# TensorE transposes are placed between the products of a group instead of behind it, in a fused GroupNorm, Hadamard and two-layer-MLP kernel

## The chip, the cores and the metric

One core of one Trainium2 chip. The time is device time in microseconds (us), the median of the runs of one kernel. PE is TensorE, ACT is ScalarE, DVE is VectorE and POOL is GpSimd. Each engine runs its own list of instructions in order and waits on semaphores; data in transit lies in PSUM banks, which PE writes and ACT and DVE read.

## The reference

The input x has shape (16, 192, 56, 56), float32. Two residual blocks follow each other; each normalises over 32 groups of 6 channels and then mixes the channels of every pixel.

```python
def _gn(v, G=32, eps=1e-05):
    B_, C_, H_, W_ = v.shape
    g = v.reshape(B_, G, C_ // G, H_, W_)
    m = jnp.mean(g, axis=(2, 3, 4), keepdims=True)
    s = jnp.var(g, axis=(2, 3, 4), keepdims=True)
    return ((g - m) / jnp.sqrt(s + eps)).reshape(v.shape)
...
x = x + _L0_conv_ref(_gn(x))      # y = xr padded to 256 @ hadamard / 16, first 192 columns
x = x + _L1_conv_ref(_gn(x), W1, b1, g1, beta1, W2, b2, g2, beta2, W3, b3)
...
# _L1_conv_ref, for each pixel, over its 192 channels:
h = jnp.einsum('bhwc,oc->bhwo', h, W1) + b1
h = jax.nn.gelu(_layernorm(h, g1, beta1), approximate=False)
h = jnp.einsum('bhwc,oc->bhwo', h, W2) + b2
h = jax.nn.gelu(_layernorm(h, g2, beta2), approximate=False)
h = jnp.einsum('bhwc,oc->bhwo', h, W3) + b3
```

## The kernel before, in words

Images are taken in 8 pairs. The 3136 pixels of a pair are cut into six units of 512 pixels; the 64 left over of each are collected into one more unit (g = 44), so there are 49. A unit holds 2 x 192 channels in three blocks of 128 partitions: a and b (128 channels of either image) and c (64 of each). Every float32 operand of a product is split into a float16 high and low part, so a product is two or three matmuls.

A unit goes through these pieces on PE, each a function of its code:

- `h_ab`, `h_c` (and `h_left` for the leftovers): Hadamard products, 512 columns wide, into the PSUM tile `hl` (banks "a" and "b"). DVE adds them to x (`residual`, L1089; `residual_left`, L1098).
- `group(g, n, h)`: layer n (0 or 1) of the MLP for half h of unit g: two bias products of 388 columns (L567), 12 pairs of 192 columns on 64 rows each (L573), 12 of 192 columns on 128 rows (L578), into `tm[h]`. Its output has pixels on the partitions. ACT squares it and sums the squares (L729), POOL makes the reciprocal root (L935), DVE multiplies (`normalise`, L1248) into `z[n]`.
- `transposes(g, n, h)`: six float32 transposes of 128 x 128 of `z[n]` (four, L590, into bank "tp0"; two, L597, into "tp1"), which bring the channels back to the partitions. The code calls layer 1 n = 0 and layer 2 n = 1. The first four wait until ACT has read what bank tp0 held. ACT applies gelu (L741 from tp0, L746 from tp1 after the second half) and makes the high part (`gelu_hi`, L759); POOL makes the low part (`gelu_lo`, L943).
- `l3_ab`, `l3_c`: the third product, 512 columns, again into `hl`. DVE adds it to x (`final_ab`, L1279; `final_c`, L1287), and it is stored. `l3_ab` waits for `gelu_lo` of the unit; `l3_c` waits until `final_ab` has read bank "a" (its first product is L511, its last L516).

`run` calls one function for each g on every engine: `first` for g below 6, `step` up to 41, `last` up to 47, `drain` for the rest. A step works on several units at once: layer 1 of unit g, layer 2 of unit g-1, the third product of unit g-2, the Hadamard product of unit g+7. Each sixth step collects statistics for a GroupNorm (`gn_means`, `h_shift`, `w1_shift`: small products into bank "b", with short DVE operations round them).

The lists of the other engines are fixed in the same way. In a step, ACT has: squares(g,0,0), gelu(g-2,1,1), the first high part of the next Hadamard input (xs_hi), gelu_hi(g-2,1,1), squares(g,0,1), two more xs_hi, squares(g-1,1,0), gelu(g,0,0), three high parts of the next layer 1 input (x_hi, L706), gelu_hi(g,0,0), squares(g-1,1,1), gelu(g,0,1), gelu_hi(g,0,1), gelu(g-1,1,0), gelu_hi(g-1,1,0). DVE has: statistics of x, residual, normalise(g,0,0), two more residuals with statistics, two xs_lo, normalise(g,0,1), one xs_lo, two low parts of the layer 1 input (L1230), final_ab(g-2), normalise(g-1,1,0), the third low part, statistics, normalise(g-1,1,1), final_c(g-2). POOL has: the root for (g,0,0), gelu_lo(g-2,1,1), roots for (g,0,1) and (g-1,1,0), gelu_lo(g,0,0), the root for (g-1,1,1), gelu_lo(g,0,1), gelu_lo(g-1,1,0).

## Time and profile before

| | |
|---|---|
| median of 3 runs | 927.61 us (927.29 to 929.92) |
| span of the profiled execution | 927.5 us |
| PE busy | 831.8 us, 90% |
| ACT busy | 814.3 us, 88% |
| DVE busy | 799.5 us, 86% |
| POOL busy | 551.2 us, 59% |
| granted TensorE clock, mean | 0.985 of full speed |

The profiled execution is one run with the profiler on; its own time is its span, within 0.1 us of the median, with nothing listed around it. A line such as "412.65 0.34 PE L567 ... x2" says that two instructions of line 567 start at 412.65 us and that the last ends 0.34 later. Matmuls are pipelined, so a matmul's duration is longer than the distance to the next one; the distance of starts is what a matmul costs.

### The profile page before, as it was taken

What the parts mean: (1) busy time and instruction counts of PE and PEld (TensorE: products, weight loads), DVE (VectorE), ACT (ScalarE), POOL (GpSimd) and SP (SyncE); (2) the same over time, 40 slices, a digit from 0 to 9 for tenths busy, and PEclk for the clock granted to TensorE, in tenths of its full rate; (3) what the DMA queues carried; (4) which work ended last, traced back from release to release, by engine and by line L of the source; (5) the groups of instructions that cost most, each with busy time, mean ns of one, the idle gap of its engine ahead of it and who ended that gap; (6) DMA issues with size and microseconds to landing.
All of it is one profiled execution on the core that took longest, in us unless ns stands there. A gap on an engine that the chain in (4) does not pass through costs nothing.

```text
span 927.5 us, 22221 instructions
## 1 busy us (share of the span) xinstructions
PE 831.8 (90%) x8353; PEld 552.3 (60%) x8353; DVE 799.5 (86%) x1416; ACT 814.3 (88%) x2400; POOL 551.2 (59%) x414
## 2 busy tenths in 40 slices
PE   0646889899999999999999999999999999889897
PEld 0114545556666666666666666666666667566663
DVE  6699898999999999999999999999998887745455
ACT  0687879689999999999999999999999998999982
POOL 0452544566666666666666666766766666577760
PEclk9987999999999999999999999999999999999999
DMA  9725022223323333233233232332111113121213
GB/s 265 234 69 145 1 70 69 74 69 104 107 69 108 103 105 98 81 103 108 70 110 101 94 117 70 98 113 84 59 40 55 50 36 104 40 69 35 70 36 102
DMA packets 52090, 81.99 MB, mean 88 GB/s; under 512 B 14608, under 2 KB 14736, under 8 KB 51856
## 3 DMA queue, kind: packets, MB, share of 16 engines
q1 hardware_dynamic: 51984, 80.58, 28.8%
q8 instruction: 67, 1.10, 0.5%
q14 instruction: 39, 0.32, 0.1%
HBM read 41.23 MB, written 39.32 MB: 87 GB/s over the span
## 4 chain that ended last, share of the span: by engine, by line
PE 48%; DVE 31%; ACT 10%; POOL 7%; issue 2%; SPq 1%; DMA 1%; ACTq 0%; DVEq 0%; POOLq 0%
PE tm L578 11%; DVE z L1248 6%; PE tm L573 5%; PE tp L590 5%; DVE X L1089 5%; DVE xs_lo L1080 4%; POOL ge_lo L943 4%; PE hl L487 4%; DVE bn L1106 3%; DVE x_lo L1230 3%; PE hl L418 3%; ACT z L729 3%; PE tm L567 3%; PE hl L516 2%; PE hl L492 2%; PE hl L511 2%
## 5 line engine op out<-in xcount | busy, mean ns | idle before, releaser
L943 POOL TENSOR_TENSOR ge_lo<-ge,ge_hi 128x512 f16<-128x512 f32 (+1 forms) x190 | 314.1, 1664 | 189.7 <-ACT ge_hi L759 189.7
L729 ACT ACTIVATE z<-tm 128x194 f32<-128x194 f32 x784 | 250.8, 346 | 41.9 <-PE tm L578 38.6
L935 POOL TENSOR_TENSOR rs<-ssq,neg_half 128x4 f32<-128x4 f32 x196 | 204.9, 1046 | 124.1 <-ACT z L729 123.2
L1248 DVE TENSOR_TENSOR z<-tm,rs 128x768 f32<-128x768 f32 x196 | 186.0, 949 | 62.1 <-POOL rs L935 61.3
L729 ACT ACTIVATION_READ_ACCUMULATOR z<-tm 128x1 f32 x784 | 175.1, 223 | 0.0
L741 ACT ACTIVATE ge<-tp,par 128x512 f32<-128x512 f32 x196 | 155.2, 792 | 21.1 <-PE tp L590 20.5
L759 ACT ACTIVATE ge_hi<-ge 128x512 f16<-128x512 f32 (+1 forms) x190 | 161.8, 855 | 2.9
L1089 DVE SCALAR_TENSOR_TENSOR X<-hl,h_bias,X 128x512 f32<-128x512 f32 x138 | 102.0, 741 | 30.6 <-PE hl L423 30.1
L590 PE MATMUL tp<-cst,z 128*128 128x128 f32 x784 | 121.8, 278 | 4.9 <-DVE z L1248 2.8
L1230 DVE SCALAR_TENSOR_TENSOR x_lo<-X,gscale,x_hi 128x512 f16<-128x512 f32 x144 | 102.8, 743 | 1.1 <-ACT x_hi L706 1.1
L590 PEld LDWEIGHTS tp<-cst,z 128*128 128x128 f32 x784 | 85.7, 142 | 28.4 <-issue 21.7
L706 ACT ACTIVATE x_hi<-X,gscale 128x512 f16<-128x512 f32 x144 | 95.7, 745 | 6.8 <-DVE gshift L1186 6.5
L578 PE MATMUL tm<-w_hi,ge_hi 128*128 128x192 f16 x392 | 98.0, 250 | 0.0
L1106 DVE BATCH_NORM_STATS2 bn<-X 128x6 f32<-128x512 f32 x144 | 97.6, 683 | 0.0
L578 PE MATMUL tm<-w_hi,ge_lo 128*128 128x192 f16 x392 | 97.0, 247 | 0.0
L578 PE MATMUL tm<-w_lo,ge_hi 128*128 128x192 f16 x392 | 97.0, 247 | 0.0
L578 PE MATMUL tm<-w_hi,x_hi 128*128 128x192 f16 x384 | 96.6, 252 | 0.0
L695 ACT ACTIVATE xs_hi<-X,gscale 128x512 f16<-128x512 f32 (+1 forms) x129 | 92.6, 767 | 4.4 <-DVE gscale L1177 4.4
L578 PE MATMUL tm<-w_lo,x_hi 128*128 128x192 f16 x384 | 95.7, 249 | 0.0
L578 PE MATMUL tm<-w_hi,x_lo 128*128 128x192 f16 x384 | 95.6, 249 | 0.0
L1080 DVE SCALAR_TENSOR_TENSOR xs_lo<-X,gscale,xs_hi 128x512 f16<-128x512 f32 (+1 forms) x129 | 92.9, 751 | 0.5 <-ACT xs_hi L695 0.4
L1066 DVE BATCH_NORM_STATS2 bn<-X 128x6 f32<-128x512 f32 x132 | 83.4, 677 | 4.8 <-DMA X<-x 4.7
(192 smaller groups left out, 1888.2 us busy)
## 6 DMA issues: line engine op xcount, KB each, us to landing
out<-X SPq DMA_DIRECT2D x48, 512.0 KB, 2.9
X<-x SPq DMA_DIRECT2D x40, 512.0 KB, 4.0
out<-X SPq DMA_DIRECT2D x98, 128.0 KB, 3.0
X<-x SPq DMA_DIRECT2D x80, 128.0 KB, 4.1
X<-x SPq DMA_DIRECT2D x8, 576.0 KB, 4.2
X<-x SPq DMA_DIRECT2D x16, 144.0 KB, 4.4
X<-weights SPq DMA_DIRECT2D x1, 1024.0 KB, 12.1
out<-X SPq DMA_DIRECT2D x8, 64.0 KB, 3.0
```

The lines of the kernel that those rows point to most:

```text
L578: last = nc.tensor.matmul(dst[:, i, k * TW:k * TW + C], tokens(act, slice(0, 128), i, k), w[:, 3 * i, :], start=False, stop=(r == 2), skip ...
L590: last = nc.tensor.transpose(tp[:, 0, i * HALF + k * TT:i * HALF + (k + 1) * TT], z[n][:, 2 * h + k, at:at + 128], ident[0:TT, 0:TT])
L729: last = nc.scalar.activation(z[n][:, 2 * h + k, i * TW:(i + 1) * TW], tm[h][:, i, k * TW:(k + 1) * TW], ACT.Square, scale=float(C) ** -0. ...
L741: nc.scalar.activation(ge[n][:, 2 * h:2 * h + 2, :], tp[:, 0, 0:2 * HALF].rearrange("p (b t) -> p b t", b=2), ACT.Gelu, bias=par[:, 4 * n ...
L759: nc.scalar.activation(ge_hi[n][:, g % 2, PART[h], :], ge[n][:, PART[h], :], ACT.Copy).then_inc(s_ge_hi[n], 1)
L935: nc.gpsimd.tensor_tensor(rs[n][:, 2 * h:2 * h + 2, :], ssq[n][:, 2 * h:2 * h + 2, :], neg_half[0:TT, 0:4].rearrange("p (i k) -> p i k", i=2),
L943: nc.gpsimd.tensor_tensor(ge_lo[n][:, g % 2, PART[h], :], ge[n][:, PART[h], :], ge_hi[n][:, g % 2, PART[h], :], ALU.subtract).then_inc(s_g ...
L1080: ins = nc.vector.scalar_tensor_tensor(out=xs_at(xs_lo, a, wide(a))[:, b, :], in0=xcols(a, b, wide(a)), scalar=scale1(a // U, b), in1=xs_a ...
L1089: nc.vector.scalar_tensor_tensor(out=xcols(a, b), in0=tp[:, 0, 0:UT] if b == 2 and a < U else hl[:, b % 2, 0:UT], scalar=h_bias[:, (a // U ...
L1106: ins = nc.vector.bn_stats(bn[1][:, (a // U) % 2, b, a % U, :], xcols(a, b))
L1230: ins = nc.vector.scalar_tensor_tensor(out=x1_lo[:, a % 2, b, :], in0=xcols(a, b), scalar=scale2(a // U, b), in1=x1_hi[:, a % 2, b, :], op ...
L1248: nc.vector.tensor_tensor(z[n][:, 2 * h:2 * h + 2, 0:2 * C].rearrange("p k (i o) -> p i k o", i=2), tm[h][:, :, 0:2 * TW].rearrange("p i ( ...
```

## The change

A new function `transpose(g, n, h, j)` does the j-th of the six transposes of `transposes(g, n, h)`, with the same waits and signals: the wait for z and for bank tp0 before the first, the signal to ACT after the fourth. `group`, `h_ab`, `l3_ab` and `l3_c` take a second set of numbers, `turned`, and place those six transposes between their own products. ACT, DVE, POOL and SP keep their lists. The lines of `drain` change only where g is 48; `first` leaves out its last transposes when g is 5, since step 6 now makes them.

```diff
-            def h_ab(a):
+            def h_ab(a, *turned):
...
                         nc.tensor.matmul(hl[:, i, 0:UT], h16[:, AA, :], part[:, i, :], start=(r == 0), stop=False,
                                          skip_group_check=True)
+                        if turned:
+                            transpose(*turned, 2 * i + r)
+                if turned:
+                    transposes(*turned, 4)
...
-            def l3_ab(g):
+            def l3_ab(g, *turned):
...
                         nc.tensor.matmul(dst[:, i], w[:, AA, :], act[:, i:4:2, :], start=(r == 0), stop=False,
                                          skip_group_check=True)
+                        if turned:
+                            transpose(*turned, 3 * i + r)
...
-            def l3_c(g):
+            def l3_c(g, *turned):
...
                     nc.tensor.matmul(dst, w[:, CCB, :], act[:, 4:6, :], start=(r == 0), stop=False,
                                      skip_group_check=True)
+                    if turned:
+                        transpose(*turned, 2 * r)
+                        transpose(*turned, 2 * r + 1)
...
-            def group(g, n, h):
+            def group(g, n, h, *turned):
...
+                            if turned and (3 * k + r) % 2 == 1 and (i, k, r) != (0, 1, 2):
+                                transpose(*turned, 3 * i + (3 * k + r) // 2)
                     last.then_inc(s_mm[n], 1)
-
-            def transposes(g, n, h):
+                    if turned and i == 0:
+                        transpose(*turned, 2)
+
+            def transpose(g, n, h, j):
+
+
+
                 if not 0 <= g < NL:
                     return
...
+                if j == 0:
+                    pe.wait_ge(s_z[n], 2 * g + h + 1)
+                    free("tp0")
+                if j < 4:
+                    k, i = divmod(j, 2)
+                    at = (0, C + CC)[i]
+                    last = nc.tensor.transpose(tp[:, 0, i * HALF + k * TT:i * HALF + (k + 1) * TT],
+                                               z[n][:, 2 * h + k, at:at + 128], ident[0:TT, 0:TT])
+                    if j == 3:
+                        last.then_inc(s_tp[n], 1)
+                        held["tp0"] = s_ge[n], 3 * g + h + 1
+                    return
+                k = j - 4
+                if k == 0 and h == 0:
                     free("tp1")
...
+            def transposes(g, n, h, first=0):
+                for j in range(first, 6):
+                    transpose(g, n, h, j)
...
             def step(g):
-                group(g, 0, 0)
-                transposes(g - 2, 1, 1)
-                h_ab(h_unit(g, 0))
+                group(g, 0, 0, g - 2, 1, 0)
+                h_ab(h_unit(g, 0), g - 2, 1, 1)
                 group(g, 0, 1)
...
                 h_left(h_unit(g, 0))
-                transposes(g, 0, 0)
-                l3_ab(g - 2)
+                l3_ab(g - 2, g, 0, 0)
                 group(g - 1, 1, 1)
-                transposes(g, 0, 1)
                 w1_shift(gn2_pair(g))
                 h_shift(h_shift_pair(g))
-                l3_c(g - 2)
-                transposes(g - 1, 1, 0)
+                l3_c(g - 2, g, 0, 1)
 
             def last(g):
-                group(g, 0, 0)
+                group(g, 0, 0, g - 2, 1, 0)
                 transposes(g - 2, 1, 1)
                 group(g, 0, 1)
                 group(g - 1, 1, 0)
-                transposes(g, 0, 0)
-                l3_ab(g - 2)
+                l3_ab(g - 2, g, 0, 0)
                 group(g - 1, 1, 1)
-                transposes(g, 0, 1)
-                l3_c(g - 2)
-                transposes(g - 1, 1, 0)
+                l3_c(g - 2, g, 0, 1)
```

The first place, on PE: the end of a plain step, from the last products of layer 2 to the first of the next unit's group. Before (L590 and L597 are transposes, L511 and L516 are l3_c, L567 is the next group):

```order
L578 MATMUL tm<-w_hi,ge_lo 128x192
L590 MATMUL tp<-cst,z 128x128 x4
L597 MATMUL tp<-cst,z 128x128 x2
L511 MATMUL hl<-ge_hi,w_hi 128x512
L511 MATMUL hl<-ge_lo,w_hi 128x512
L511 MATMUL hl<-ge_hi,w_lo 128x512
L516 MATMUL hl<-ge_hi,w_hi 64x512 x2
L516 MATMUL hl<-ge_lo,w_hi 64x512 x2
L516 MATMUL hl<-ge_hi,w_lo 64x512 x2
L590 MATMUL tp<-cst,z 128x128 x4
L597 MATMUL tp<-cst,z 128x128 x2
L567 MATMUL tm<-bias,ones 128x388 x2
```

The same place of the changed kernel (L619 and L628 are the transposes, L526 and L534 are l3_c, L588 the next group; in this step a w1_shift stands ahead):

```order
L526 MATMUL hl<-ge_hi,w_hi 128x512
L619 MATMUL tp<-cst,z 128x128 x2
L526 MATMUL hl<-ge_lo,w_hi 128x512
L619 MATMUL tp<-cst,z 128x128 x2
L526 MATMUL hl<-ge_hi,w_lo 128x512
L628 MATMUL tp<-cst,z 128x128 x2
L534 MATMUL hl<-ge_hi,w_hi 64x512 x2
L534 MATMUL hl<-ge_lo,w_hi 64x512 x2
L534 MATMUL hl<-ge_hi,w_lo 64x512 x2
L588 MATMUL tm<-bias,ones 128x388 x2
```

The six of layer 1's second half moved from ahead of l3_c to behind its first product; the six of layer 2 that stood between l3_c and the next group are gone from here.

The second place, on PE: the second part of group(g,0,0) and the start of h_ab. Before, the twelve L578 stood in a row, then six transposes, then h_ab:

```order
L578 MATMUL tm<-w_lo,x_hi 128x192
L578 MATMUL tm<-w_hi,x_lo 128x192
L590 MATMUL tp<-cst,z 128x128 x4
L597 MATMUL tp<-cst,z 128x128 x2
L418 MATMUL hl<-xs_hi,h 128x512
L418 MATMUL hl<-xs_lo,h 128x512
```

Now the last six of the twelve (L599), with four transposes among and before them, and then h_ab (L421):

```order
L619 MATMUL tp<-cst,z 128x128
L599 MATMUL tm<-w_hi,x_hi 128x192
L599 MATMUL tm<-w_lo,x_hi 128x192
L619 MATMUL tp<-cst,z 128x128
L599 MATMUL tm<-w_hi,x_lo 128x192
L599 MATMUL tm<-w_hi,x_hi 128x192
L628 MATMUL tp<-cst,z 128x128
L599 MATMUL tm<-w_lo,x_hi 128x192
L599 MATMUL tm<-w_hi,x_lo 128x192
L628 MATMUL tp<-cst,z 128x128
L421 MATMUL hl<-xs_hi,h 128x512
L619 MATMUL tp<-cst,z 128x128
```

Between the products of group(g,0,0) stand the six of layer 2's first half, which were behind l3_c; the six of its second half, which followed the group, now alternate with h_ab's four wide products.

The third place, on PE: l3_ab (L497), where six transposes (L619, L628) of layer 1's first half stood ahead of its first product and now alternate with it:

```order
L599 MATMUL tm<-w_hi,ge_lo 128x192
L497 MATMUL hl<-ge_hi,w_hi 128x512
L619 MATMUL tp<-cst,z 128x128
L497 MATMUL hl<-ge_lo,w_hi 128x512
L619 MATMUL tp<-cst,z 128x128
L497 MATMUL hl<-ge_hi,w_lo 128x512
L619 MATMUL tp<-cst,z 128x128
L497 MATMUL hl<-ge_hi,w_hi 128x512
L619 MATMUL tp<-cst,z 128x128
L497 MATMUL hl<-ge_lo,w_hi 128x512
```

The wait of l3_ab for POOL's low part now stands ahead of these transposes too.

## Rows read from the trace of the kernel before

**Rows 1.** The page: busy time, share of the span and instructions of each engine.
```profile
PE 831.8 (90%) x8353; PEld 552.3 (60%) x8353; DVE 799.5 (86%) x1416; ACT 814.3 (88%) x2400; POOL 551.2 (59%) x414
```

**Rows 2.** Waits of DVE, 190 to 720 us (us in total, times, longest).
```profile
DVE X L1089 <- PE hl L423: 15.9, 16, 2.9
```

**Rows 3.** Line L1279 over the span: who waited for it (us, times).
```profile
  PEld hl L511: 6.5, 16
```

**Rows 4.** Timeline of PE: first products of group(g,0,0) (start us, us, what).
```profile
412.65 0.34 PE L567 MATMUL tm<-bias,ones 64*128 64x388 f16 x2
...
428.65 0.34 PE L567 MATMUL tm<-bias,ones 64*128 64x388 f16 x2
...
444.54 0.34 PE L567 MATMUL tm<-bias,ones 64*128 64x388 f16 x2
...
462.01 0.34 PE L567 MATMUL tm<-bias,ones 64*128 64x388 f16 x2
...
479.25 0.34 PE L567 MATMUL tm<-bias,ones 64*128 64x388 f16 x2
...
497.77 0.34 PE L567 MATMUL tm<-bias,ones 64*128 64x388 f16 x2
...
844.19 0.34 PE L567 MATMUL tm<-bias,ones 64*128 64x388 f16 x2
...
859.34 0.34 PE L567 MATMUL tm<-bias,ones 64*128 64x388 f16 x2
```

**Rows 5.** Timeline of DVE, steps 19 and 22.
```profile
416.68 0.75 DVE L1089 SCALAR_TENSOR_TENSOR X<-hl,h_bias,X 128x512 f32<-128x512 f32 x1 [0.48 <-PE hl L423]
...
423.73 0.74 DVE L1230 SCALAR_TENSOR_TENSOR x_lo<-X,gscale,x_hi 128x512 f16<-128x512 f32 x1
...
425.05 1.21 DVE L1279 SCALAR_TENSOR_TENSOR X<-hl,X 128x1024 f32<-128x1024 f32 x1
...
471.47 0.66 DVE L1098 SCALAR_TENSOR_TENSOR X<-hl,h_bias,X 128x64 f32<-128x64 f32 x3
...
474.89 1.22 DVE L1279 SCALAR_TENSOR_TENSOR X<-hl,X 128x1024 f32<-128x1024 f32 x1
```

**Rows 6.** Timeline of PE, end of step 18 and step 19.
```profile
409.68 0.60 PE L590 MATMUL tp<-cst,z 128*128 128x128 f32 x4
...
410.33 0.38 PE L511 MATMUL hl<-ge_hi,w_hi 128*128 128x512 f16 x1
410.55 0.38 PE L511 MATMUL hl<-ge_lo,w_hi 128*128 128x512 f16 x1
...
411.53 0.38 PE L516 MATMUL hl<-ge_hi,w_lo 128*64 128x512 f16 x2
411.84 0.66 PE L590 MATMUL tp<-cst,z 128*128 128x128 f32 x4
412.34 0.38 PE L597 MATMUL tp<-cst,z 128*128 128x128 f32 x2
...
413.42 0.26 PE L578 MATMUL tm<-w_hi,x_hi 128*128 128x192 f16 x1
...
414.42 0.60 PE L590 MATMUL tp<-cst,z 128*128 128x128 f32 x4
...
419.31 0.34 PE L567 MATMUL tm<-bias,ones 64*128 64x388 f16 x2
```

**Rows 7.** Timeline of ACT and of POOL, step 19.
```profile
413.08 0.76 ACT L741 ACTIVATE ge<-tp,par 128x512 f32<-128x512 f32 x1
...
417.57 1.08 ACT L759 ACTIVATE ge_hi<-ge 128x1024 f16<-128x1024 f32 x1
...
422.17 0.86 ACT L741 ACTIVATE ge<-tp,par 128x512 f32<-128x512 f32 x1
...
422.83 0.81 ACT L706 ACTIVATE x_hi<-X,gscale 128x512 f16<-128x512 f32 x1
...
418.72 2.13 POOL L943 TENSOR_TENSOR ge_lo<-ge,ge_hi 128x1024 f16<-128x1024 f32 x1 [1.25 <-ACT ge_hi L759]
```

More of the change, by code:

```diff
@@ L584, in transposes @@
                     return
-                pe.wait_ge(s_z[n], 2 * g + h + 1)
-                done = 3 * g + h
-                free("tp0")
-                for k in range(2):
-                    for i, at in ((0, 0), (1, C + CC)):
-                        last = nc.tensor.transpose(tp[:, 0, i * HALF + k * TT:i * HALF + (k + 1) * TT],
-                                                   z[n][:, 2 * h + k, at:at + 128], ident[0:TT, 0:TT])
-                last.then_inc(s_tp[n], 1)
-                held["tp0"] = s_ge[n], done + 1
@@ L595, in transposes @@
+                k = j - 4
+                if k == 0 and h == 0:
                     free("tp1")
-                for k in range(2):
-                    last = nc.tensor.transpose(tp[:, 1, h * HALF + k * TT:h * HALF + (k + 1) * TT], z[n][:, 2 * h + k, CA:CA + 128],
-                                               ident[0:TT, 0:TT])
-                if h == 1:
+                last = nc.tensor.transpose(tp[:, 1, h * HALF + k * TT:h * HALF + (k + 1) * TT], z[n][:, 2 * h + k, CA:CA + 128],
+                                           ident[0:TT, 0:TT])
@@ L600, in transposes @@
+                if k == 1 and h == 1:
                     last.then_inc(s_tp[n], 1)
-                    held["tp1"] = s_ge[n], done + 2
+                    held["tp1"] = s_ge[n], 3 * g + 3
+            def transposes(g, n, h, first=0):
+                for j in range(first, 6):
+                    transpose(g, n, h, j)
             def first(g):
```

17 lines of the change are left out of this document (14 added, 3 removed).

## The prediction, written before the changed kernel was run

> **What bounds the kernel now.** I read the page first. PE, ACT and DVE are all busy for 86 to 90% of the span [rows 1], so shares alone name no bound. The reader should see there only that a gain on PE alone may be worth nothing.
>
> Then the waits. In the stretch of full steps (190 to 720 us) DVE has one wait of weight: for the last product of h_ab, before the first residual of a step, 15.9 us in 16 waits [rows 2]. The other side is in the waits of l3_c: its first weight load (L511) waits for final_ab (L1279) 16 times [rows 3]. So the two engines hand a baton round: PE's h_ab releases DVE's residual, DVE runs without a gap to final_ab, final_ab releases l3_c, and PE runs from l3_c through group(g,0,0) to the next h_ab.
>
> The timelines of one step show that this loop closes. I call S the start of group(g,0,0); step 19 has S = 412.65, and the next has 428.65, 16.00 later [rows 4]. Residual starts at S+4.03, final_ab ends at 425.05+1.21 = S+13.61 [rows 5]. In the step before, final_ab's waiter L511 starts at 410.33, 2.32 before S [rows 6]. 4.03 + 9.58 + 0.06 of handing over (L511 would start at S+13.67) + 2.32 = 15.99: the step. There is no slack in it. ACT is the other full engine: from the gelu at 413.08 on it has no gap in this step [rows 7].
>
> Of six steps (one pair of images) three are plain; the two of them in the rows last 16.00 and 15.89. The other three carry GroupNorm work and last 17.47, 17.24 and 18.52 [rows 4].
>
> **The cost of a transpose.** Six transposes before a 512-column product take 410.33 - 409.68 = 0.65, so 0.109 each; a 512-column product takes 0.217 (410.33 to 410.55), and twelve 192-column ones 1.00 (413.42 to 414.42), 0.083 each [rows 6]. A 512-column product behind a change of array shape (from 128 rows and columns to 64 rows or 64 columns, or back) comes 0.31 after the one before it, so a change costs 0.09. Four transposes behind such a change take 0.50 instead of 0.44 (411.84 to 412.34): an exposed float32 weight load costs 0.06. That is less than any product beside it, so the loads are hidden already, and alternating hides nothing more. The last of the six before L511 also keeps its 0.109 though a float16 load stands behind it, whereas 192-column products follow such loads at 0.083. I price an alternated transpose at 0.109. No row shows one between 512-column products; the bounds are 0.05 (if 0.06 is all that it needs) and 0.17 (0.109 plus an exposed load).
>
> The Trainium skill, "TensorE: Matmul & The Clock Gate", section "LDWEIGHTS (loading the stationary operand)", gives columns/1.2 ns, an estimate of 107 ns for these 128 columns: then transposes in a row are bound by their loads and alternating would pay. The row of the exposed load speaks against it; it is the third rival.
>
> **What the change saves.** The six transposes between l3_c and group(g,0,0) go. From the last pair of L516 (411.53) to S is 1.12 now; without them one change of array shape stays, priced as the one seen (411.53 to 411.84, 0.31). 1.12 - 0.31 - 0.65 (the six are done elsewhere) = 0.16 saved a step. If PE were the bound, 42 steps would give 7 us.
>
> **What it puts on the loop.** (1) transposes(g,0,1), 0.65, ran before l3_c's wait for final_ab, hidden. Now they stand behind l3_c's first product, so behind that wait. l3_c to S: 2.32 + 0.65 - 0.81 = 2.16. (2) The six that stood before S now stand inside group(g,0,0): h_ab, and with it the residual, comes at S+4.68, not 4.03. Together +0.49 a step. If DVE had a gap before final_ab, this would be covered; it has none.
>
> (3) Bank tp0. The gelu of transposes(g-2,1,0) must finish before transposes(g-2,1,1) may begin. Before, a whole group(g,0,0) stood between them. Now the fourth of the first six starts at S + 0.77 + 8 x 0.083 + 3 x 0.109 = S+1.76, ends 0.27 later (0.60 for four less three starts), ACT's gelu starts 0.05 behind that, at S+2.08, and lasts 0.76 [rows 7], and PE may go on at S+2.9. PE gets there at S + 0.77 + 1.00 + 0.65 + 0.22 = S+2.64. Stall and exposed load: 0.33. DVE is late next: residual at S+5.01.
>
> (4) ACT's queue. That gelu stood at 413.08 = S+0.43; now it can't be before S+2.08, and everything behind it in ACT's order follows at its old distance, since ACT has no gap. gelu_hi(g-2,1,1) started 4.49 after it (417.57), GpSimd's gelu_lo 5.64 after it and took 2.13 (418.72 to 420.85) [rows 7]. So l3_ab can't start before 2.08 + 7.77 + 0.06 = S+9.91; PE is there at S+9.41: group(g-1,1,0) starts at 419.31 = S+6.66 now, later by 0.65 and 0.33, and takes 1.77 (as 412.65 to 414.42 does). Stall 0.5, where now gelu_lo ends at 420.85 = S+8.2 and l3_ab starts at 6.66 + 1.77 + 0.65 = S+9.08.
>
> (5) transposes(g,0,0) ran before l3_ab and its wait; now they alternate with it. The fourth starts at 9.91 + 4 x 0.217 + 3 x 0.109 = S+11.11; 0.32 later, as in (3), gelu(g,0,0) starts, at S+11.43 (now 422.17 = S+9.52). Behind it in ACT's queue stand the three x_hi splits, 0.66 later (422.17 to 422.83) [rows 7], the first done 0.81 after its start, at S+12.90. DVE's x1 low parts (L1230) wait for it: they start at S+12.95 (now 423.73 = S+11.08; the loop alone would give 12.06). From there to the end of final_ab is 425.05 + 1.21 - 423.73 = 2.53 [rows 5], so l3_c starts at 12.95 + 2.53 + 0.06 = S+15.54 and the next step at +2.16: 17.7. A plain step goes from 15.9 to 17.7, +1.8. DVE's idle moves from the residual to x1_lo and POOL's chain; ACT gets gaps.
>
> The step with h_left (17.24): l3_ab there also waits for the leftover residual (L1098, 471.47 = S+9.46, three in 0.66) [rows 5]. That now comes at about 9.46 + 0.98 + 0.66 + 0.05 = S+11.15, and transposes(g,0,0) stand behind it: gelu at S+12.67, x_hi done at 14.14, final_ab at 14.19 + 2.53 = 16.72, then h_shift, which holds l3_c back by 17.24 - (474.89 + 1.22 - 462.01) - 2.32 = 0.82 [rows 4, 5] beyond final_ab, and 2.16: about 19.75, +2.5. In the other two, DVE has 1.5 to 2.6 us more of its own work in the step, which covers part of ACT's delay: between 0 and the plain 1.8; I take 0.75 each, about (1) to (3) alone.
>
> Six steps: 3 x 1.8 + 2.5 + 2 x 0.75 = 9.4. Steps 7 to 38 are 5.33 such sixes: 50. Steps 6 and 39 to 42 lie in between, one each: 5. The last plain ones (43 to 47, 844.19 to 859.34 = 15.15 [rows 4]) have no h work, but (3) and (4) hold on a loop of their own: l3_c to S 2.16, gelu 2.08, to gelu_lo's end and on 7.4 (7.83 less the xs split that ACT no longer has in between, some 0.4), l3_ab 2.7 (nine slots of 0.217, a change, six transposes), group(g-1,1,1) 1.77: 16.1, +0.9 each: 4. First steps (0 to 5) hardly change. Sum: +59. The profiled span is 927.5, 0.1 under the median of the runs, so I add to the median: 927.6 + 59, 986 us in whole numbers.
>
> **Rivals.**
> Second: (1) to (3) hold, but (4) and (5) are absorbed, because ACT's list has more give than one step shows. Then five of six steps gain 0.82 and one 0.1: 4.2 per six, 22, and 4 at the ends: 954. For it speaks that (4) and (5) are long sums of which each term must hold, and that ACT could gain a little where its operations are queued closely; against, that ACT shows no gap and its order is fixed.
> Third: alternated transposes cost 0.05, as if the load had been their price. 18 of them stand on loop (1) and (2), 12 on the way through (5): 0.65 less a step, 42 steps, 27 us less than the forecast: 959. That is where the page's rule would lead. Faster than before it does not become, since waits 3 to 5 stay.
> Fourth: only +0.49 holds, since gelu comes back in time: 2.5 per six and a little: 943.
> Fifth, other side: PE is the bound in practice and DVE catches up, because its waits before the residual (15.9 us) are slack and not part of the loop. Then 0.16 x 42 remain: 921. It decides if final_ab comes 0.65 earlier relative to PE; L511's 16 waits and the sum 15.99 speak against it.
> Sixth: the two cancel: 928.
>
> **How the numbers follow.** Chances: forecast 0.58, second 0.20, third 0.07, fourth 0.05, fifth 0.06, sixth 0.04. The forecast's own range is 968 to 1000 (each special step at its bounds, a transpose at up to 0.17). The range for all leaves out the fourth to sixth (0.15) and the upper tail: 945 to 997. A difference of 0.3% is about what can be told from no change. Slower 0.90, same 0.04, faster 0.06.
>
> **What the profile after would show.** Plain steps of 17.7, not 15.9. (1) L526 (l3_c) waiting for final_ab in nearly every step, for 1 us or more. (2) residual at S+5.0. (3) PE waiting about 0.3 for ACT's gelu in h_ab. (4) l3_ab waiting for GpSimd. (5) DVE waiting for x_hi before L1230. Transposes 0.109 after a 512-column product. Wrong would be: plain steps under 16.4, L526 without waits, or transposes at 0.05.

## The result, and the profile after

The kernel after takes 1001.42 us (median of 4 runs, 1000.71 to 1001.99) where the kernel before takes 927.45 beside it (926.90 to 929.92). The ratio is 1.079, 95% interval 1.077 to 1.081: 74 us slower. The forecast was 986 and the range 945 to 997, so the time lies outside it. The direction and most of the size came as written, and 15 us are left to explain.

The page of the kernel after: busy time and share of each engine, then the shares of the chain that ended last.

```profile
PE 839.8 (84%) x8353; PEld 569.8 (57%) x8353; DVE 822.9 (82%) x1416; ACT 821.8 (82%) x2400; POOL 560.7 (56%) x414
...
PE 33%; DVE 29%; ACT 19%; POOL 12%; issue 4%; SPq 1%; DMA 1%; ACTq 0%; DVEq 0%; POOLq 0%
```

Against [rows 1], no engine has much more work; all three full ones are idle for longer. DVE alone has 23 us more of busy time with the same 1416 instructions: some of them take longer than before, and the prediction had no such term.

Line numbers moved: h_ab is L421 and L430, l3_ab L497 and L504, l3_c L526 and L534, the group L588 to L599, the transposes L619 (tp0) and L628 (tp1), the gelu L773, x_hi L738, the residual L1121, the copy of GroupNorm means L1194, x1's low part (x_lo) L1262, final_ab L1311; POOL's root is L967, its gelu_lo L975. In the single-part kernels the numbers differ by one to three.

The waits, in the stretch 190 to 720 us (engine, line and who it waited for: us in total, times, longest):

```profile
ACT ge L773 <- PE tp L619: 65.5, 71, 3.1
DVE X L1121 <- PE hl L430: 28.2, 20, 2.7
...
PEld hl L526 <- DVE X L1311: 22.8, 20, 1.3
...
DVE x_lo L1262 <- ACT x_hi L738: 10.6, 9, 1.5
...
DVE z L1280 <- POOL rs L967: 5.6, 15, 2.3
...
PE hl L497 <- DVE gmu L1194: 4.4, 5, 0.9
PE hl L497 <- POOL ge_lo L975: 4.0, 14, 0.3
```

The reader sees ACT, which had no gap in step 19 [rows 7], wait 71 times for the transposes (6 times and 4.9 us in the kernel before); l3_c wait for final_ab by about 1.1 us each; and DVE's wait before the residual grow from 15.9 to 28.2 us [rows 2]. The 9 waits for x_hi stand one in each GN1 step (0.88) and one in each h_left step (1.54), none in a plain step; the kinds of step are explained at the table below. The last three rows are 15 waits for POOL's root (one, 0.6 us, in the kernel before), 5 for a copy of GroupNorm means and 14 of PE for gelu_lo; of the last two the kernel before has none.

The same plain step as in the prediction, step 19, first on PE (start us, us, what; in brackets the idle time before it and who ended it). S is 436.38.

```profile
436.38 0.34 PE L588 MATMUL tm<-bias,ones 64*128 64x388 f16 x2
...
439.38 0.30 PE L619 MATMUL tp<-cst,z 128*128 128x128 f32 x1 [0.20 <-ACT ge L773]
...
446.30 0.39 PE L497 MATMUL hl<-ge_hi,w_hi 128*128 128x512 f16 x1 [0.28 <-POOL ge_lo L975]
446.52 0.27 PE L619 MATMUL tp<-cst,z 128*128 128x128 f32 x1
446.63 0.38 PE L497 MATMUL hl<-ge_lo,w_hi 128*128 128x512 f16 x1
...
451.84 0.39 PE L526 MATMUL hl<-ge_hi,w_hi 128*128 128x512 f16 x1 [0.90 <-DVE X L1311]
...
454.01 0.34 PE L588 MATMUL tm<-bias,ones 64*128 64x388 f16 x2
```

The step is 454.01 - 436.38 = 17.63 long; it was 16.00 [rows 4]. A transpose between 512-column products costs 446.63 - 446.52 = 0.11, no less and no more than in a row [rows 6].

The other engines in the same step:

```profile
438.46 0.78 ACT L773 ACTIVATE ge<-tp,par 128x512 f32<-128x512 f32 x1 [0.64 <-PE tp L619]
...
447.81 0.78 ACT L773 ACTIVATE ge<-tp,par 128x512 f32<-128x512 f32 x1
448.49 1.94 ACT L738 ACTIVATE x_hi<-X,gscale 128x512 f16<-128x512 f32 x3
...
444.11 2.13 POOL L975 TENSOR_TENSOR ge_lo<-ge,ge_hi 128x1024 f16<-128x1024 f32 x1 [1.88 <-ACT ge_hi L791]
446.20 1.46 POOL L967 TENSOR_TENSOR rs<-ssq,neg_half 128x4 f32<-128x4 f32 x1
...
441.46 0.75 DVE L1121 SCALAR_TENSOR_TENSOR X<-hl,h_bias,X 128x512 f32<-128x512 f32 x1 [1.34 <-PE hl L430]
...
445.65 1.80 DVE L1112 SCALAR_TENSOR_TENSOR xs_lo<-X,gscale,xs_hi 128x512 f16<-128x512 f32 x2
447.69 0.96 DVE L1280 TENSOR_TENSOR z<-tm,rs 128x768 f32<-128x768 f32 x1 [0.23 <-POOL rs L967]
...
449.23 1.42 DVE L1262 SCALAR_TENSOR_TENSOR x_lo<-X,gscale,x_hi 128x512 f16<-128x512 f32 x2
```

Taken off S: the gelu at +2.08, the residual at +5.08, l3_ab at +9.92, the second gelu at +11.43, x1's low part at +12.85, l3_c at +15.46. Two of DVE's rows were not forecast. The pair of xs_lo takes 1.80 (1.40 in the kernel before), and the normalise behind it waits for a root that takes 1.46 and not 1.01.

Steps of all kernels, measured between first products of group(g,0,0) as in [rows 4]. "GN1" and "GN2" are the two steps of six that the prediction calls "the other two": GN1 collects the statistics for the first GroupNorm (steps 21, 27 and so on), GN2 those for the second (steps 23, 29). "Held" counts the xs_lo of over 0.9 us, of 153. Each ratio is to the kernel before as run beside that kernel, whose median lay between 927.45 and 929.21.

```
kernel       median   ratio [95%]             plain  GN1    h_left  GN2    43-47  held
before       927.45                           15.92  17.47  17.24   18.52  15.15    0
after       1001.42   1.079 [1.077, 1.081]    17.63  19.18  19.78   20.16  16.08   28
only_l3c     955.07   1.028 [1.025, 1.030]    16.77  17.63  17.63   19.42  15.30    0
only_l3ab    946.37   1.019 [1.017, 1.021]    16.28  18.44  18.42   18.68  15.23    0
only_g00     964.46   1.038 [1.036, 1.040]    16.97  17.56  17.98   19.90  15.43   23
only_hab     942.21   1.014 [1.011, 1.016]    16.39  17.47  17.93   18.93  15.16   23
undo_l3c     981.48   1.057 [1.055, 1.060]    16.99  18.55  19.13   19.91  16.10   23
undo_l3ab    988.94   1.066 [1.064, 1.067]    17.63  18.22  18.16   20.17  16.05   28
block_all    977.76   1.053 [1.051, 1.055]    17.10  18.61  19.25   19.54  15.47    0
early_xslo   933.59   1.006 [1.005, 1.008]    16.11  17.48  17.61   18.53  15.15   23
hab_clear    954.15   1.026 [1.024, 1.029]    17.02  17.48  18.30   19.50  15.16    5
block_only   944.15   1.016 [1.014, 1.017]    16.36  17.48  17.35   19.30  15.16   16
after_gn     998.06   1.074 [1.072, 1.075]    17.64  18.16  19.79   20.19  16.09   23
```

(Plain of before is the mean of 15.86, 16.00 and 15.89; plain of hab_clear is that of steps 18 and 19.)

### The profile page after: what moved, and what is told of

Its sections match the earlier page's. It is cut to its first block, busy times and chain, and to the rows that moved or that the text cites. A ratio compares the mean times of both kernels' runs of the same rounds, so it can differ in the third digit from the quotient of the medians.

```text
span 1000.2 us, 22221 instructions
## 1 busy us (share of the span) xinstructions
PE 839.8 (84%) x8353; PEld 569.8 (57%) x8353; DVE 822.9 (82%) x1416; ACT 821.8 (82%) x2400; POOL 560.7 (56%) x414
## 4 chain that ended last, share of the span: by engine, by line
PE 33%; DVE 29%; ACT 19%; POOL 12%; issue 4%; SPq 1%; DMA 1%; ACTq 0%; DVEq 0%; POOLq 0%
POOL ge_lo L975 7%; PE tm L599 6%; DVE x_lo L1262 6%; ACT ge L773 5%; ACT z L761 5%; PE tp L619 5%; DVE xs_lo L1112 5%; DVE X L1311 5%; POOL rs L967 5%; DVE z L1280 5%; PE tm L594 4%; PE hl L526 3%; PE hl L534 3%; ACT ge_hi L791 3%; PE hl L497 2%
## 5 line engine op out<-in xcount | busy, mean ns | idle before, releaser
L975 POOL TENSOR_TENSOR ge_lo<-ge,ge_hi 128x512 f16<-128x512 f32 (+1 forms) x190 | 312.1, 1654 | 280.5 <-ACT ge_hi L791 280.5
L967 POOL TENSOR_TENSOR rs<-ssq,neg_half 128x4 f32<-128x4 f32 x196 | 215.1, 1098 | 99.0 <-ACT z L761 93.1
L773 ACT ACTIVATE ge<-tp,par 128x512 f32<-128x512 f32 x196 | 153.2, 782 | 104.6 <-PE tp L619 103.4
L619 PE MATMUL tp<-cst,z 128*128 128x128 f32 x784 | 185.7, 276 | 14.6 <-ACT ge L773 13.7
L1121 DVE SCALAR_TENSOR_TENSOR X<-hl,h_bias,X 128x512 f32<-128x512 f32 x138 | 102.0, 741 | 52.6 <-PE hl L430 52.4
L619 PEld LDWEIGHTS tp<-cst,z 128*128 128x128 f32 x784 | 106.0, 141 | 41.8 <-issue 27.0
L1262 DVE SCALAR_TENSOR_TENSOR x_lo<-X,gscale,x_hi 128x512 f16<-128x512 f32 x144 | 103.1, 745 | 15.1 <-ACT x_hi L738 14.9
L1112 DVE SCALAR_TENSOR_TENSOR xs_lo<-X,gscale,xs_hi 128x512 f16<-128x512 f32 (+1 forms) x129 | 105.0, 843 | 1.2 <-ACT xs_hi L727 1.0
L738 ACT ACTIVATE x_hi<-X,gscale 128x512 f16<-128x512 f32 x144 | 94.4, 715 | 7.8 <-DVE gshift L1218 7.8
L599 PE MATMUL tm<-w_hi,ge_hi 128*128 128x192 f16 x392 | 98.0, 250 | 0.0
L1138 DVE BATCH_NORM_STATS2 bn<-X 128x6 f32<-128x512 f32 x144 | 97.6, 683 | 0.0
L599 PE MATMUL tm<-w_hi,ge_lo 128*128 128x192 f16 x392 | 96.9, 247 | 0.0
L599 PE MATMUL tm<-w_lo,ge_hi 128*128 128x192 f16 x392 | 96.9, 247 | 0.0
L599 PE MATMUL tm<-w_hi,x_hi 128*128 128x192 f16 x384 | 96.4, 251 | 0.0
L599 PE MATMUL tm<-w_hi,x_lo 128*128 128x192 f16 x384 | 95.4, 249 | 0.0
L599 PE MATMUL tm<-w_lo,x_hi 128*128 128x192 f16 x384 | 95.4, 249 | 0.0
L628 PE MATMUL tp<-cst,z 128*128 128x128 f32 x392 | 89.0, 273 | 0.0
```

Of the source, the lines that this page charges most:

```text
L599: last = nc.tensor.matmul(dst[:, i, k * TW:k * TW + C], tokens(act, slice(0, 128), i, k), w[:, 3 * i, :], start=False, stop=(r == 2), skip ...
L619: last = nc.tensor.transpose(tp[:, 0, i * HALF + k * TT:i * HALF + (k + 1) * TT], z[n][:, 2 * h + k, at:at + 128], ident[0:TT, 0:TT])
L773: nc.scalar.activation(ge[n][:, 2 * h:2 * h + 2, :], tp[:, 0, 0:2 * HALF].rearrange("p (b t) -> p b t", b=2), ACT.Gelu, bias=par[:, 4 * n ...
L967: nc.gpsimd.tensor_tensor(rs[n][:, 2 * h:2 * h + 2, :], ssq[n][:, 2 * h:2 * h + 2, :], neg_half[0:TT, 0:4].rearrange("p (i k) -> p i k", i=2),
L975: nc.gpsimd.tensor_tensor(ge_lo[n][:, g % 2, PART[h], :], ge[n][:, PART[h], :], ge_hi[n][:, g % 2, PART[h], :], ALU.subtract).then_inc(s_g ...
L1112: ins = nc.vector.scalar_tensor_tensor(out=xs_at(xs_lo, a, wide(a))[:, b, :], in0=xcols(a, b, wide(a)), scalar=scale1(a // U, b), in1=xs_a ...
```

## The experiments

**Each part alone.** Four kernels take the kernel before and one place of the change. The diffs show `step`; `last` has the same edit where it has these lines.

```diff
 # only_l3c
-                transposes(g, 0, 1)
...
-                l3_c(g - 2)
+                l3_c(g - 2, g, 0, 1)
 # only_l3ab
-                transposes(g, 0, 0)
-                l3_ab(g - 2)
+                l3_ab(g - 2, g, 0, 0)
 # only_g00 (and the six behind l3_c go)
-                group(g, 0, 0)
+                group(g, 0, 0, g - 2, 1, 0)
 # only_hab
-                transposes(g - 2, 1, 1)
-                h_ab(h_unit(g, 0))
+                h_ab(h_unit(g, 0), g - 2, 1, 1)
```

> Only the six transposes of layer 1's second half alternate with l3_c; the other three groups of six stay where the kernel before has them. Loop theory: these six now stand behind l3_c's wait for final_ab, and that wait ends each step's loop in the kernel before, so each of the 33 steps with index 6 to 38 and the few after it is longer by 0.65 to 0.7 us: plain steps 16.6, 955 us (950 to 960). Theory that alternating itself is dear on PE (the 74 us lost are spread over the four alternated groups alike): 946 us, and transposes further apart than 0.109 us behind a 512-column product. Theory that the waits do not matter: 928.

> Only the six of layer 1's first half alternate with l3_ab. Loop theory: gelu(g,0,0) comes 0.4 us later, and behind it in ACT's list x_hi, for which DVE's low part waits before final_ab: plain steps 16.3; the step with h_left +1.7, because the six now stand behind the leftover residual; the step with gn1 statistics +0.4, the one with gn2 statistics 0. Sum some 20 us: 948 (940 to 954). Theory that alternating itself is dear: 946, with all six kinds of step longer by the same 0.4.

> Only the first six of layer 2 move from behind l3_c into group(g,0,0); the other three groups stay in a row. Loop theory: one change of array shape less (0.16 saved), but h_ab comes 0.65 later, PE waits some 0.5 for bank tp0, and ACT's gelu can't start before 2.08 us after the step's start, which delays POOL's low part, POOL's root and DVE's normalise: plain steps 16.8 to 17.0, 967 us (960 to 975). Theory that alternating itself is dear: 946 or less. Theory that PE's own work is the bound: 921.

> Only the six of layer 2's second half alternate with h_ab; h_ab starts 0.65 earlier and ends when it did. Loop theory: no transpose moves behind a wait that binds, only gelu(g-2,1,1) comes 0.3 us later, and with it ACT's list: plain steps 16.0 to 16.2, 934 us (928 to 940), the smallest of the four. Theory that alternating itself is dear: 946.

Measured: 955.07, 946.37, 964.46 and 942.21. The first three are within 3 us of what was expected: putting six transposes behind l3_c's wait, behind l3_ab's wait, or ahead of a gelu that must come early, each costs time by itself. Alternating with h_ab, which has no such wait in front, was expected to cost least and did, but cost twice the expected: 942, not 934, and outside the 928 to 940 that was given. The four add up to 26 + 17 + 35 + 13 = 91 us against 74 together, so they share part of their cost.

**The miss of only_hab.** Its plain step, DVE and POOL:

```profile
421.48 0.75 DVE L1123 SCALAR_TENSOR_TENSOR X<-hl,h_bias,X 128x512 f32<-128x512 f32 x1 [0.45 <-PE hl L430]
...
425.52 1.62 DVE L1114 SCALAR_TENSOR_TENSOR xs_lo<-X,gscale,xs_hi 128x512 f16<-128x512 f32 x2
427.38 0.96 DVE L1282 TENSOR_TENSOR z<-tm,rs 128x768 f32<-128x768 f32 x1 [0.24 <-POOL rs L969]
...
430.24 1.22 DVE L1313 SCALAR_TENSOR_TENSOR X<-hl,X 128x1024 f32<-128x1024 f32 x1
...
423.80 2.14 POOL L977 TENSOR_TENSOR ge_lo<-ge,ge_hi 128x1024 f16<-128x1024 f32 x1 [1.75 <-ACT ge_hi L793]
425.89 1.46 POOL L969 TENSOR_TENSOR rs<-ssq,neg_half 128x4 f32<-128x4 f32 x1
```

From the residual's start to final_ab's end DVE needs 430.24 + 1.22 - 421.48 = 9.98, where it needed 9.58 before. The first xs_lo starts at 425.52, inside a gelu_lo that ends at 425.94. The root starts while that xs_lo runs and takes 1.46. In the kernel before, the gelu_lo ended (420.85 [rows 7]) before the pair began:

```profile
420.88 1.40 DVE L1080 SCALAR_TENSOR_TENSOR xs_lo<-X,gscale,xs_hi 128x512 f16<-128x512 f32 x2
```

So the pair takes 0.22 longer in only_hab, 1.62 for 1.40. The theory: an xs_lo and a POOL operation exclude each other, and the later one waits. The next kernel makes only that collision, with no transpose moved.

```diff
 # early_xslo: the kernel before, and in DVE's list
-                stats_x1(h_unit(g, 0), 1)
                 scaled_lo(xs_unit(g, 0), 0)
+                stats_x1(h_unit(g, 0), 1)
```

> The kernel before with two neighbours on DVE swapped in each full step: the first low part of the Hadamard input (xs_lo, two inputs in SBUF) stands ahead of the second statistics of x1, so it starts 0.6 us earlier, while POOL's gelu_lo still runs. Nothing is moved on PE, ACT or POOL. Theory that these two shut each other out: xs_lo takes 1.1 to 1.3 instead of 0.74 in most steps, POOL's root behind it 1.4, plain steps 16.3, 942 us (935 to 948). Theory that the long xs_lo of the changed kernel have another cause: 928.

```profile
421.17 1.02 DVE L1115 SCALAR_TENSOR_TENSOR xs_lo<-X,gscale,xs_hi 128x512 f16<-128x512 f32 x1
...
419.51 2.13 POOL L978 TENSOR_TENSOR ge_lo<-ge,ge_hi 128x1024 f16<-128x1024 f32 x1 [1.25 <-ACT ge_hi L794]
421.60 1.46 POOL L970 TENSOR_TENSOR rs<-ssq,neg_half 128x4 f32<-128x4 f32 x1
```

Same operations, same shapes: xs_lo goes from 0.74 to 1.02 (0.98 to 1.14) and the root behind it from 1.01 to 1.46, in 23 steps. The collision is real, and its whole price on this loop is 0.2 a plain step and 0.6% in all. I had expected 942 (935 to 948), 14 us over the kernel before, and it is 5.4 over the 928.15 beside it: I had the cause right and its size some 2.5 times too large.

The converse was tried on only_hab: DVE's third group of statistics goes from the step's start, where DVE waits, to just ahead of the first xs_lo, so that xs_lo starts behind gelu_lo.

```diff
 # hab_clear: only_hab, and in DVE's list
-                stats_part(g, 2)
...
                 stats_x1(h_unit(g, 0), 1)
+                if gn1_pair(g) is None:
+                    stats_part(g, 2)
                 scaled_lo(xs_unit(g, 0), 0)
```

> The kernel with only h_ab's alternation, and one more edit: DVE's third stats_part, 0.60 us, is taken from the step's start, where DVE waits, and put just ahead of the first xs_lo (except in the steps with statistics of GroupNorm 1, which need it). So xs_lo starts 0.60 later, behind the end of GpSimd's gelu_lo and the start of the root. If an xs_lo that starts inside a gelu_lo is what holds both back, then xs_lo falls from 0.96 to 0.74, the root from 1.46 to 1.01, and DVE's way from the residual to final_ab is 9.58 + 0.60 = 10.18 where it was 9.98 with the hold: plain steps of 16.6, about 948 in all, slower than 942 because the loop now carries work that the wait had covered. The rival, that gelu_lo and the root are only late and slow by themselves, keeps both durations and gives 9.98 + 0.60: plain steps of 17.0, about 958.

```profile
426.82 0.75 DVE L1123 SCALAR_TENSOR_TENSOR X<-hl,h_bias,X 128x512 f32<-128x512 f32 x1 [1.64 <-PE hl L430]
...
430.86 1.27 DVE L1100 BATCH_NORM_STATS2 bn<-X 128x6 f32<-128x512 f32 x2
432.05 1.40 DVE L1114 SCALAR_TENSOR_TENSOR xs_lo<-X,gscale,xs_hi 128x512 f16<-128x512 f32 x2
...
436.22 1.22 DVE L1313 SCALAR_TENSOR_TENSOR X<-hl,X 128x1024 f32<-128x1024 f32 x1
...
431.23 1.01 POOL L969 TENSOR_TENSOR rs<-ssq,neg_half 128x4 f32<-128x4 f32 x1
```

The kernel takes 954.15, between the 948 of the theory and the 958 of the rival. The step came out at 17.02, the rival's figure, but not for the rival's reason. The durations are those of the theory: the root behind gelu_lo is 1.01 again and the pair of xs_lo takes 1.40 again. What I had wrong is the work moved: two statistics, 432.05 - 430.86 = 1.19, not 0.60. From the first xs_lo to normalise it is now 433.36 - 432.05 = 1.31, where only_hab has 427.38 - 425.52 = 1.86, which holds the longer xs_lo and the wait for the root. DVE's way is 10.62 = 9.98 + 1.19 - 0.55. In step 20, where one statistic is moved, the step is 16.43: 0.60 of work more on the loop and 0.04 of time, so 0.56 was given back there. The edit doesn't keep every root clear: in step 19 the next one starts inside the pair of xs_lo (432.86) and takes 1.45, and nothing waits for it.

**Taking one part back.** Two kernels are the kernel after with l3_c or l3_ab as before.

```diff
 # undo_l3c: the kernel after, and
+                transposes(g, 0, 1)
...
-                l3_c(g - 2, g, 0, 1)
+                l3_c(g - 2)
 # undo_l3ab: the kernel after, and
-                l3_ab(g - 2, g, 0, 0)
+                transposes(g, 0, 0)
+                l3_ab(g - 2)
```

> The changed kernel with one part undone: the six of layer 1's second half stand in a row ahead of l3_c again. Loop theory: 0.65 a step leaves the stretch from l3_c's wait to the next step: plain steps 17.0 (17.63 in the changed kernel), 975 us (970 to 980). Theory that the parts overlap and another loop takes over: 990 or more.

> The changed kernel with one part undone: the six of layer 1's first half stand in a row ahead of l3_ab again. Loop theory: in a plain step POOL's chain (gelu_hi, gelu_lo, the root, normalise) ends as late as before, so plain steps stay at 17.5 to 17.6; the step with h_left falls from 19.8 to about 18.3, the one with gn1 statistics by 0.5 to 1. Together 988 us (983 to 994). Theory that the four parts simply add (this part alone cost 17 us): 984.

Measured 981.48 and 988.94, the first a little over the 970 to 980 that was expected. Without l3_c's part a plain, GN1 or h_left step is 0.63 to 0.65 shorter, GN2 only 0.25, and the last ones (43 to 47) not at all: there another path ends as late. Without l3_ab's part the plain step does not move by a hundredth (17.63), GN2 neither, but GN1 loses 0.96 and h_left 1.62. So transposes(g,0,0) behind l3_ab's wait, step (5) of the prediction, decide GN1 and h_left and not the plain steps. That agrees with the kernel after, where DVE waits for x_hi in GN1 and h_left alone. What decides the plain steps is in the chain of the last work of undo_l3ab (start us, us, what):

```profile
435.05 0.79 ACT ge L775
...
439.68 0.95 ACT ge_hi L793
...
440.71 2.14 POOL ge_lo L977
442.84 1.43 POOL rs L969
```

Gelu late, gelu_hi late, gelu_lo late, then the root that is held behind xs_lo, then (444.29) normalise and final_ab. In the kernel after this chain and the one through l3_ab and x_hi end together: the first x_hi starts at 448.49 and takes 0.71, and DVE comes to x1's low part at 449.23 without a wait.

**The same transposes in a row.** block_all keeps each six at its new place, but puts those of group(g,0,0) in a row between the 64-row and the 128-row products.

```diff
 # block_all: the kernel after, and in group(g, n, h)
+                if turned:
+                    transposes(*turned)
                 for i in range(2):
                     for k in range(2):
...
-                            if turned and (3 * k + r) % 2 == 1 and (i, k, r) != (0, 1, 2):
-                                transpose(*turned, 3 * i + (3 * k + r) // 2)
```

> The changed kernel, but the first six of layer 2 stand in a row between the 64-row and the 128-row products of group(g,0,0), not among the latter; all else as changed. Their fourth is 0.66 us earlier, h_ab is not. Loop theory: gelu(g-2,1,0) starts at 1.42 instead of 2.08 us into the step, PE no longer waits for bank tp0 in h_ab, plain steps 17.0, 975 us (968 to 982). Theory that only where h_ab and l3_c stand counts, and not when ACT gets its work: at most 0.33 a step, 988 or more.

Measured 977.76. The fourth transpose starts eight 192-column products earlier, 8 x 0.083 = 0.66 by [rows 6], the gelu with it, and the plain step falls by 0.53. Of that, 0.35 is the residual, at S+4.73 for S+5.08, since h_ab no longer waits for bank tp0; the other 0.18 is DVE's way from there to final_ab (10.14 for 10.32), on which no xs_lo is held. PE needs as long as before from S to h_ab (2.47, and 2.42 in the kernel after). So among these products alternating brings nothing, and being late costs.

**Only the block, on the kernel before.** It removes one change of the array's shape a step, and nothing else.

```diff
 # block_only: the kernel before, with block_all's group(g, n, h), and in step
-                group(g, 0, 0)
+                group(g, 0, 0, g - 2, 1, 0)
...
-                transposes(g - 1, 1, 0)
```

> The kernel before, with one change: layer 2's first six transposes stand in a row inside group(g,0,0), between its 64-row and its 128-row products, where the array's shape changes anyway, and so no longer between l3_c and the group. One change of array shape goes, 0.16 a step. The fourth transpose starts at S + 0.77 + 3 x 0.109, so that gelu starts at S+1.42 and ends 0.2 before PE needs the bank: no stall. If the loop PE to DVE to PE alone set the time, plain steps would be 15.83, and the kernel 921 to 926. ACT's gelu however comes 1.0 later in the step (S+1.42, was S+0.43), and gelu_lo and x_hi behind it with 15.99 us of ACT's work in a step of 16: against that, plain steps of 16.1 to 16.5 and 928 to 945. I take the second, 934, since the alternated form of the same move alone (964) cost more than its loop did.

Measured 944.15, ratio 1.016, at the upper end of the 928 to 945 that was expected: plain 16.36 and GN2 19.30. In step 19 l3_c to S is 1.53 (2.32 before) and the residual comes at S+4.73 (4.03 before), so PE's share of the loop is 0.09 shorter. DVE's way from the residual to final_ab is 10.05 (9.58 before):

```profile
410.96 1.70 DVE L1115 SCALAR_TENSOR_TENSOR xs_lo<-X,gscale,xs_hi 128x512 f16<-128x512 f32 x2
```

The gelu comes 1.0 later, gelu_lo with it; it holds this pair (7 more xs_lo of this kernel took 0.85 to 0.90, under the bound of the table), and normalise waits for a root of 1.46. Making PE's share shorter and giving ACT its gelu later makes the kernel 1.6% slower. That is the trade of the whole change in its smallest form, and it adds no alternation at all.

**The two GroupNorm steps.** In GN1 of the kernel after, the prediction's l3_ab at S+9.91 came at 483.13 - 471.64 = S+11.49. PE and DVE there, and last one row of DVE in GN2:

```profile
471.64 0.34 PE L588 MATMUL tm<-bias,ones 64*128 64x388 f16 x2
...
480.91 2.00 DVE L1112 SCALAR_TENSOR_TENSOR xs_lo<-X,gscale,xs_hi 128x576 f16<-128x576 f32 x2
482.83 0.15 DVE L1194 COPY gmu<-hl 128x8 f32<-128x8 f32 x1
...
483.13 0.38 PE L497 MATMUL hl<-ge_hi,w_hi 128*128 128x512 f16 x1 [0.87 <-DVE gmu L1194]
...
519.60 0.89 DVE L1197 TENSOR_TENSOR gsq<-gmu 128x4 f32<-128x4 f32 x1
```

l3_ab writes the PSUM bank in which the means of GroupNorm lie, and waits until DVE has copied them out; the copy stands behind two xs_lo, of which the first is held (2.00 for the pair). In GN2, the square of those means, 128 x 4 numbers, took 0.89 us where it took 0.16 (the row at 487.20 of the kernel before, below). after_gn mends both.

```diff
 # after_gn: the kernel after, and in gn_var
+                means = gp[:, 0:8].rearrange("p (k s i) -> p k s i", k=2, s=2)
+                do(nc.vector.tensor_copy(gmu[:, :, :].rearrange("p s (k i) -> p k s i", k=2), means))
+                nc.vector.tensor_tensor(gsq[:, :].rearrange("p (k i) -> p k i", k=2),
+                                        gmu[:, 0, :].rearrange("p (k i) -> p k i", k=2), means[:, :, 0, :], ALU.mult
+                                        ).then_inc(s_gread, 1)
...
-                do(nc.vector.tensor_tensor(gsq[:, :], gmu[:, 0, :], gmu[:, 0, :], ALU.mult))
 # and in DVE's list
                 stats_x1(h_unit(g, 0), 1)
+                gn_var(gn1_pair(g), 0)
                 scaled_lo(xs_unit(g, 0), 0)
                 scaled_lo(xs_unit(g, 0), 1)
                 residual_left(h_unit(g, 0))
-                gn_var(gn1_pair(g), 0)
```

> The kernel after, with two edits in DVE's GroupNorm work, for the two steps of six that came out larger than forecast. (a) In the step with GroupNorm 1 (19.18), l3_ab waited for DVE's copy of the means out of hl, which stood behind two xs_lo held by gelu_lo (2.00 for 1.52); the copy now stands ahead of them. Expected: l3_ab 0.87 earlier, the step 18.3 to 18.5. (b) In the step with GroupNorm 2 (20.16), the square of the means, 128x4, took 0.89 where it took 0.16 before, since it started inside a gelu_lo with two operands in SBUF; now it reads one of them from PSUM. Expected: 0.16 to 0.25, the step 19.4 to 19.6. Plain steps stay 17.63. In all 6 x 0.8 + 6 x 0.65 less: 992. If the two steps are long because DVE's own work there is just longer than I took it, neither edit changes anything: 1000 to 1001.

Measured 998.06, where 992 was expected. GN1 is 18.16, a little under the expected 18.3: its l3_ab has no wait left, and the cause is shown. GN2 is 20.19, not shorter at all, although the square now takes 0.16 each time. Its rows, DVE and POOL of after_gn:

```profile
516.77 0.16 DVE L1196 TENSOR_TENSOR gsq<-gmu,hl 128x4 f32<-128x4 f32 x1
516.97 0.70 DVE L1200 TENSOR_TENSOR gvar<-gmu,gsq 128x4 f32<-128x4 f32 x1
...
520.02 0.15 DVE L1211 COPY gscale<-gscale 64x1 f32<-64x1 f32 x1 [0.24 <-POOL gscale L959]
...
515.52 2.13 POOL L975 TENSOR_TENSOR ge_lo<-ge,ge_hi 128x1024 f16<-128x1024 f32 x1 [1.88 <-ACT ge_hi L791]
517.60 1.01 POOL L967 TENSOR_TENSOR rs<-ssq,neg_half 128x4 f32<-128x4 f32 x1
518.58 1.40 POOL L959 TENSOR_TENSOR gscale<-gvar,neg_half 128x4 f32<-128x4 f32 x1
```

The hold moved to the next operation, and it never mattered: POOL's list has gelu_lo, a root, then the GroupNorm scale, which DVE needs before it can normalise. In the kernel before, GN2 (step 23, S at 479.25 [rows 4]) had, on DVE and POOL:

```profile
487.20 0.16 DVE L1165 TENSOR_TENSOR gsq<-gmu 128x4 f32<-128x4 f32 x1
...
489.68 0.15 DVE L1177 COPY gscale<-gscale 64x1 f32<-64x1 f32 x1
...
485.12 2.14 POOL L943 TENSOR_TENSOR ge_lo<-ge,ge_hi 128x1024 f16<-128x1024 f32 x1 [1.25 <-ACT ge_hi L759]
```

gelu_lo ended there at S+8.01 and DVE's copy of the scale started at S+10.43. In after_gn, with S at 507.78, they are at S+9.87 and S+12.24, 1.86 and 1.81 later. Less the 0.16 that l3_c to S is shorter, 1.81 gives 1.65; the step is 1.67 longer. I tried no kernel with that delay alone taken away; block_all and block_only, whose gelu comes earlier, have 19.54 and 19.30, which fits.

## Why the prediction fell short

The forecast's own range ended at 1000; the one given for all cases leaves out an upper tail and ended at 997, and 1001 is outside both. Most of the steps stand, on their rows. The transposes cost 0.11 among the 512-column products too, as in a row (the third rival falls). (1) l3_c to S: 2.17 for 2.16. (2, 3) the gelu at S+2.08, as forecast, and the residual at S+5.08 for 5.01. (4) l3_ab at S+9.92 for 9.91. (5) gelu at S+11.43, as forecast. Plain steps 17.63 for 17.7, h_left 19.78 for 19.75 (its own terms, 16.72 + 0.82 + 2.16, give 19.70), the last ones 16.08 for 16.1. Of the five signs it named, the residual's place, PE's wait for the gelu (0.20, and the load behind it) and l3_ab's wait for gelu_lo came. L526 waits for final_ab in every plain and GN1 step and in no h_left or GN2 step. DVE waits for x_hi in the GN1 and h_left steps alone.

The sum by its own terms, against the profiled executions (steps 0 to 48):

```
                                   forecast   measured
plain steps of 7 to 38                28.8       29.2
h_left steps of 7 to 38               13.3       12.7
the other two, GN1 and GN2             8.0       16.7   (8.56 + 8.14)
steps 6 and 39 to 42                   5          9.0
steps 43 to 47, and 48                 4          5.7   (4.61 + 1.10)
steps 0 to 5                           0          1.8
sum                                   59         75.1
```

(The span grew by 72.7, since the first step began 2.5 earlier in that execution, and the medians by 74.)

**The term that was mis-sized** is "In the other two, DVE has 1.5 to 2.6 us more of its own work in the step, which covers part of ACT's delay ... I take 0.75 each". They measured 1.71 and 1.63 each: 16.7 us for the 8.0 of the sum. The reasoning was that more work on DVE means more slack for ACT. It does not, because the delay does not come back to DVE through x_hi alone. In GN1 it comes through the copy of the means, which holds l3_ab and the transposes behind it: after_gn took 1.02 of it back, and undo_l3ab 0.96. In GN2 the rows have it come through POOL's list, where the scale of GroupNorm stands behind gelu_lo; no run took that alone away, so for GN2 the cause is read and not shown. The upper bound of that term, 1.8, was right, and I chose a value below its middle on an argument that no row carried.

**The second** is "Steps 6 and 39 to 42 lie in between, one each: 5". They cost 9.0, as much as full steps do: PE's list in them has the same moved transposes. That this is the reason was not tested. Step 48, which was left out, cost 1.1. The two terms and step 48 are 8.7 + 4.0 + 1.1 = 13.8 of the 16 us that the sum of steps missed.

Another 1.6 us go with the clock and not with the moved transposes. They lie in step 3, whose lists are the same in both kernels. In the profiled execution of the kernel after, TensorE was granted 1.2 GHz, the lower of its two levels, for 6.80 us of that step, and in that of the kernel before for 3.40; in the 4.5 us ahead of the fall PE was busy for 2.05 (2.15 of 4.6 before), and from then on all the time. The step took 22.81 at a mean granted clock of 0.850 and 21.20 at 0.919. Of the thirteen kernels five have 0.850 there and 22.81 or 22.82; the other eight have 0.919 or 0.920 and 21.18 to 21.22. So "First steps (0 to 5) hardly change" was right: without step 3 they changed by 0.2. The rest is rounding: 43 to 47 came at 0.92 each, as forecast, and five of them are 4.6, where the sum has 4.

**The plain step was right in size and incomplete in cause.** Along the loop the rows close as before: residual at S+5.08, 10.32 from there to final_ab's end (9.58 before), 0.06, and 2.17 to the next S: 17.63. The forecast had one reason for the longer way on DVE, the chain from l3_ab to x_hi to DVE. undo_l3ab takes it away and the plain step stays. A second chain, gelu_lo to the root to normalise, ends at the same time, and 0.45 of it is the stretched root. That its hold costs the kernel after nothing in a plain step, as long as the first chain is there, is a reading of the rows; no run took the hold alone out of the kernel after.

The fifth rival (PE in practice the bound) falls with the result, and block_only shows it most plainly: PE's share of the loop got shorter and the kernel slower. The second, that (4) and (5) are absorbed, is refuted by the steps themselves. Of the kernels tried none beats the kernel before.

## What to carry to other kernels

On an in-order engine a piece of work is not free because its price is hidden: six transposes cost 0.65 wherever they were put here, but in their old place they ran during a wait, and in their new one behind it, with ACT's whole list behind them. Before interleaving, ask of each moved piece which wait it used to fill and who is signalled by it, and follow the delay of that signal through every in-order list it enters, in special steps too, not only the plain one. Where a term of a sum has a bound and no row that argues for less, take the bound.
